# Graph network with five attention passes on one core: twelve places a slot for the block steps, typed products spread over them

## The chip, the cores and the metric

One NeuronCore of a Trainium2 chip runs the whole program in one launch. The metric is device time in microseconds (us); lower is better. Before the change it is 6849.43 us, the median of 3 runs (6848.14 to 6852.22).

## The reference

The inputs are 3125 nodes of 128 float32 features and 103,125 edges sorted by destination. Four graph layers run one after the other, each on relu(layernorm(x)) and each added to x:

```
L0: agg = segment_sum(edge_weight * h[src]); h' = leaky(( agg + h) W1 + b1 + (agg * h) W2 + b2)
L1: dot-product attention, 4 heads of 32, softmax over the edges of a destination, gate, layernorm
L2: GATv2 twice: score = att . leaky(xl[src] + xr[dst]); 4 heads of 32, then 1 head of 128
L3: heterogeneous transformer twice, 8 heads of 16, 8 node types, 8 edge relations:
    k, q, v = typed_linear(x, node_type, Wk | Wq | Wv)
    kw = rel_apply(k[src], edge_type, Watt);  m = rel_apply(v[src], edge_type, Wmsg)
    out = silu(typed_linear(segment_sum(softmax(kw . q[dst]) * m), node_type, Wa)), mixed with x, layernorm
```

So there is one weighted sum over the edges (pass 0) and five attention passes: pass 1 is L1, passes 2 and 3 are L2, passes 4 and 5 are L3.

## The kernel before

**Tiles, slots, passes.** The edges are cut into 830 tiles of 128, each with edges of one block of 128 destination nodes only; there are 25 blocks, so a block has 33.2 tiles on average. 16 tiles are a slot; a pass is 52 slots. In every pass POOL gathers the source rows of each tile by an indirect DMA (`gather_rows`, line 777), 830 a pass, into buffers that hold 3 slots (passes 1, 4, 5) or 4 slots (passes 2, 3). A buffer is free again when its rows are weighed (`exv_ready`).

**A slot in an attention pass** (`attention_pass`). Work on slot s overlaps the rest of slot s-1. Each engine goes through a fixed list written out in its own `slot()`:

- PE (tensor): `dst_rows` brings the destination side of four tiles to PSUM by the turned one-hots (L1280), in four groups 0 to 3; `own_rows` (L1289, GATv2 only) adds the gathered rows; `turn_scores` (L1295/L1299) turns the scores of slot s-1; `spread_drop` (L1304) and `turn_back` (L1309/L1311) serve the running softmax; `sums` (L1328) makes the per-tile sums in six units of 3 or 2 tiles (`SUMMED`).
- DVE (vector): `product` and `score` (L1098 to L1109) for the four groups; between `score` of the last group and the weighing lies the chain of scans over the slot's scores (L1115 to L1163), which waits for PE's turned scores and ScalarE's copy; `weigh` (L1176); `add` (L1188) adds sums to the accumulator.
- ACT (scalar): `keep_scores` (L1032), `open_scale` and `exps` (L1036, L1040), `exp_columns` (L1045), and in pass 3 the weighing of two of the four groups, `weigh_tiles` (L1053).
- SP (sync) loads the one-hots, their turned form and the flags, and issues the block steps' DMAs.

**Block steps.** When the last tile of a block is summed, the node work of that block follows (normalise, gate, layernorm, projections, write of the next pass's table). It is cut into steps d = 0, 1, 2 ... (classes `AfterL1`, `AfterGat`, `AfterGats`, `AfterTyped`, `AfterAll` for passes 1 to 5). A slot has `HOOKS` = 8 places on each engine, where `after.<engine>(x)` puts the step whose `first(k) + d` is x. A place is a position in the engine's instruction order, not a time. `first(k)` depends on where the block's last tile lies in its slot:

```
def first(self, k):
    s, t = divmod(last_tile(k), GT)
    return HOOKS * (s + 1) + 6 if t < ON_TIME else HOOKS * (s + 2)
```

`ON_TIME` is 11. Blocks 0 to 8 and 14 to 22 have t < 11; here they are called **early blocks** (step 0 at the seventh place of slot s+1). Blocks 9 to 13, 23 and 24 are **late blocks** (step 0 at the first place of slot s+2). Blocks are 2.07 slots apart, so each kind repeats nearly every two slots.

**Steps that matter.** Pass 3 (`AfterGats`): d = 3 statistics on DVE, d = 5 standard deviation on ACT (`deviation`, L1507: a square root and the activation table it needs), d = 6 its use on DVE (`standard`, L1513), d = 8 the turn on PE, d = 9 `by_type` on DVE (L2081), d = 11 key and value on PE (L2093), d = 12 query (L2100), d = 14, 16, 18, 20 the relation products (L2116), each taken by ACT one place later (L2138). Pass 4 (`AfterTyped`): d = 3 turn, d = 4 `by_type`, d = 5 output product (`layer_pe`, L2333), d = 12 `by_type`, d = 13 key, value and query together, d = 15 to 18 relation products.

## Time and profile before

| | |
|---|---|
| median of 3 runs | 6849.43 us |
| the profiled execution's own time | 6853.72 us |
| its span (first to last instruction) | 6851.4 us |
| busy: POOL, DVE, PE, ACT | 69%, 72%, 68%, 24% |
| mean granted TensorE clock | 0.766 |
| indirect gathers on POOL (L777) | 4980, about 0.95 us each |

The span is cut by the trace into stretches; "busy" is the time in which an engine had an instruction in it. A wait is the idle time of an engine just before an instruction, with what ended it behind the arrow. In the trace a float32 product of 128 columns shows as two records, so `x32` of L2093 is 16 products in the program.

### The profile page before, as it was taken

How to read it: one execution, taken by the hardware profiler on the slowest of the kernel's cores; microseconds unless marked ns; L12 is line 12 of the kernel's file. 1: busy time of each engine (PE TensorE's matmuls, PEld its weight loads, DVE VectorE, ACT ScalarE, POOL GpSimd, SP SyncE). 2: the span in 40 equal slices, each digit the busy share in tenths (PEclk: the TensorE clock that was granted, in tenths of full speed). 3: DMA queues.
4: the chain of work that ended last, by engine and by line, in shares of the span. 5: the costliest groups of instructions: out<-in, count | busy, mean ns of one | idle time of the engine just before them, and what ended most of it. 6: DMA issues, size and time to landing. Idle time of an engine off the chain costs nothing. (4 is left out here: it accounts for less than half of the span.)

```text
span 6851.4 us, 92813 instructions
## 1 busy us (share of the span) xinstructions
PE 4685.2 (68%) x26423; PEld 3967.3 (58%) x26423; DVE 4944.6 (72%) x14309; ACT 1666.6 (24%) x5319; POOL 4758.0 (69%) x4996
## 2 busy tenths in 40 slices
PE   2555555566666677877688788857787776676666
PEld 1444444555555466666566666646677675565655
DVE  4444443788888688888688778857777774888887
ACT  2433333122222111111133323312222221112121
POOL 3777776777777577777577777547667663777775
PEclk8676766777777788888789889967787776777777
DMA  4544444666666454545455555556667664666665
GB/s 129 171 158 162 160 159 150 209 216 211 215 210 207 128 168 156 168 156 168 135 177 189 182 164 189 170 167 223 218 223 230 211 211 129 227 219 227 219 226 157
DMA packets 407532, 1266.65 MB, mean 185 GB/s; under 512 B 128582, under 2 KB 189766, under 8 KB 320630
## 3 DMA queue, kind: packets, MB, share of 16 engines
q1 hardware_dynamic: 200000, 760.73, 30.3%
q0 software_dynamic: 199760, 495.12, 26.3%
q10 hardware_dynamic: 7270, 4.88, 0.3%
q8 instruction: 221, 3.62, 0.2%
q14 instruction: 281, 2.30, 0.1%
HBM read 1083.37 MB, written 176.98 MB: 184 GB/s over the span
## 5 line engine op out<-in xcount | busy, mean ns | idle before, releaser
L777 POOL DMA_INDIRECT gathered_rows<-table_l,arena x3048 | 2912.0, 955 | 1083.6 <-issue 911.5
L1188 DVE TENSOR_TENSOR acc<-acc,ps 128x136 f32 (+2 forms) x4160 | 1209.2, 291 | 517.4 <-PE ps L1328 354.3
L1280 PEld LDWEIGHTS ps<-dst_side,onehot_t 128*128 128x128 f32 x8320 | 1307.2, 235 | 445.7 <-issue 370.7
L1280 PE MATMUL ps<-dst_side,onehot_t 128*128 x8320 | 1416.8, 325 | 184.1 <-issue 106.9
L777 POOL DMA_INDIRECT gathered_rows<-table_l,src_rel_edges x1116 | 1061.3, 951 | 617.9 <-issue 330.6
L1328 PE MATMUL ps<-weighted_rows,onehot 128*128 128x136 f32 (+2 forms) x8320 | 1271.3, 314 | 14.8 <-DVE acc L1188 11.1
L1328 PEld LDWEIGHTS ps<-weighted_rows,onehot 128*128 128x128 f32 x8320 | 1215.4, 225 | 48.5 <-issue 38.4
L1109 DVE TENSOR_REDUCE scores<-products 128x16 f32<-128x512 f32 (+2 forms) x1040 | 711.5, 684 | 27.0
L900 PE MATMUL ps<-gathered_rows,onehot 128*128 128x128 f32 x1664 | 338.7, 367 | 473.3 <-ACT gathered_rows L837 471.4
L777 POOL DMA_INDIRECT arena<-table_l,src_rel_edges x544 | 517.9, 952 | 193.6 <-issue 161.8
L864 DVE TENSOR_TENSOR acc<-acc,ps 128x128 f32 x832 | 238.5, 287 | 535.8 <-PE ps L900 498.7
L900 PEld LDWEIGHTS ps<-gathered_rows,onehot 128*128 128x128 f32 x1664 | 292.8, 265 | 529.5 <-ACT gathered_rows L837 528.0
L1304 PE MATMUL ps<-open_node_drop,ones 64*128 64x4 f32 (+2 forms) x520 | 131.3, 323 | 513.1 <-DVE open_node_drop L1145 513.0
L1176 DVE TENSOR_TENSOR weighted_rows<-gathered_rows,ps 128x512 f32<-128x512 f32 x732 | 454.2, 679 | 5.4 <-ACT weighted_rows L1045 4.7
L1304 PEld LDWEIGHTS ps<-open_node_drop,ones 64*128 64x128 f32 (+2 forms) x520 | 111.0, 265 | 574.1 <-DVE open_node_drop L1145 570.9
L1289 PE MATMUL ps<-gathered_rows,ident 128*128 128x512 f32 x624 | 398.9, 725 | 42.7 <-DMA gathered_rows<-table_l,arena 42.6
L1104 DVE TENSOR_TENSOR products<-gathered_rows,ps 128x512 f32<-128x512 f32 x420 | 284.8, 678 | 139.0 <-DMA gathered_rows<-table_l,src_rel_edges 69.2
L837 ACT ACTIVATE gathered_rows<-gathered_rows,arena 128x128 f32<-128x128 f32 x832 | 264.9, 391 | 434.2 <-DMA gathered_rows<-table_l,arena 433.9
L777 POOL DMA_INDIRECT arena<-table_l,arena x272 | 258.6, 951 | 82.9 <-issue 80.7
L2116 PE MATMUL ps<-arena 32*128 32x256 f32 x800 | 268.9, 462 | 33.0 <-ACT arena L2138 31.3
L1309 PE MATMUL ps<-ident,exp_scores_t 64*128 64x64 f32 (+2 forms) x260 | 99.4, 382 | 272.2 <-ACT exp_scores_t L1040 272.2
L1102 DVE SCALAR_TENSOR_TENSOR products<-ps,vectors 128x512 f32<-128x512 f32 x312 | 210.8, 676 | 102.1 <-PE ps L1289 101.6
(321 smaller groups left out, 6208.1 us busy)
## 6 DMA issues: line engine op xcount, KB each, us to landing
onehot_t<-onehots_turned SPq DMA_DIRECT2D x260, 1024.0 KB
onehot<-onehots SPq DMA_DIRECT2D x260, 1024.0 KB
onehots<-onehot SPq DMA_DIRECT2D x52, 1024.0 KB, 6.6
onehots_turned<-onehot_t SPq DMA_DIRECT2D x52, 1024.0 KB, 4.3
table_l<-arena SPq DMA_DIRECT2D x50, 1024.0 KB
gathered_rows<-table_l,arena POOLq DMA_INDIRECT x3048, 2.5
segment_flags_sb<-segment_flags SPq DMA_DIRECT2D x1300, 8.2 KB
arena<-type_mask_rows SPq DMA_DIRECT2D x75, 256.0 KB
```

The lines of the kernel that those rows point to most:

```text
L777: pool.indirect_dma_start(out=home(v, t // GC)[:, t % GC, :], out_offset=None, in_=table, in_offset=bass.IndirectOffsetOnAxis(ap=index[:, ...
L837: ins = nc.scalar.activation(weighed[:, u, t, :], rv[:, u, t, :], ACT.Copy, scale=e.ewE[:, bass.ds(s * GT + t, 1)])
L900: ins = nc.tensor.matmul(ps[:, bank(u, j), g * P:g * P + D], e.oh[:, u, GC * j + g, :], weighed[:, u, GC * j + g, :], start=True, stop=True)
L1104: ins = V.tensor_tensor(out, home(v, j)[:, :, 0:D], z, ALU.mult)
L1109: V.tensor_reduce(scE[:, GC * j:GC * (j + 1), :], e.prod[:, j % 2, :].rearrange("p (g h d) -> p g h d", g=GC, h=H), AX, ALU.add).then_inc( ...
L1176: V.tensor_tensor(exvH[:, GC * j:GC * (j + 1), :, 0:hs], home(v, j)[:, :, vrow:vrow + D].rearrange("p g (h d) -> p g h d", h=H), bc(exE[:, ...
L1188: V.tensor_tensor(a, a, ps[:, BP + n % 3, at:at + PW], ALU.add).then_inc(e.acc_step.sem, 1)
L1280: ins = nc.tensor.matmul(ps[:, BZ + k, g * P:(g + 1) * P], e.ohT[:, u, t * P:(t + 1) * P], kRows[:, bass.ds(bs[t % 8], D)], start=not by_p ...
L1289: nc.tensor.matmul(ps[:, BZ + j % 2, :].rearrange("p (g d) -> p g d", d=D), e.ident[:, :], home(v, j)[:, :, 0:D], start=False, stop=True). ...
L1304: nc.tensor.matmul(dropP, e.onesF[0:LP, :], e.drop[0:LP, :, :].rearrange("p q h -> p (q h)")[:, 0:H], start=True, stop=True)\
L1328: ins = nc.tensor.matmul(ps[:, BP + n % 3, at:at + PW], e.oh[:, u, t, :], exvT[:, t, :], start=True, stop=True)
L2116: ins = mm(home, self.kvS[lane, m * P:(m + 1) * P], self.bd[lane, m * RELS * BAND:(m + 1) * RELS * BAND], start=True, stop=True)
```

## The change

`HOOKS` becomes 12: each slot has twelve places instead of eight. On PE they lie: places 0, 1 before `spread_drop`; 2 before `dst_rows` 2; 3 before the sums; 4 and 5 around `dst_rows` 3; 6 between sums units 4 and 5; 7, 8, then the first destination rows of the next slot, 9, 10 and, behind `own_rows` 3, 11. On DVE 0 and 1 precede the chain of scans, 2 the weighing, 3 `product` 1, 4 to 7 lie around the first adds, 8 after `score` 2, 9 and 10 after the adds of unit 3, 11 after `score` 3. On ACT 0 and 1 precede `open_scale`, 2 follows the weighing, 11 follows `keep_linear`. The steps keep their numbers up to the typed products; from there on they are renumbered. `first(k)` is 12 (s+1) + 9 for early blocks and 12 (s+2) for late ones. PE's `dst_rows` 0 of slot s+1 moves from the start of its slot to place 9 of slot s.

```diff
-HOOKS = 8
+HOOKS = 12
...
-                for h in range(3, 7):
+                for h in range(3, 11):
                     after.act(act, x + h)
...
-                if cur:
-                    bs = blocks_of(s, 0)
-                    e.oht_here[u].wait(pe, a_no, 16 * (q + 1))
-                    dst_rows(s, w, qw, 0, bs)
                 if chain:
                     turn_scores(r)
                 if cur:
                     own_rows(s, w, qw, 0)
-                    dst_rows(s, w, qw, 1, bs)
+                    dst_rows(s, w, qw, 1, first_places.pop(s))
...
+                after.pe(pe, x + 5)
                 if chain:
                     sums(r, v, 3)
-                after.pe(pe, x + 5)
+                    sums(r, v, 4)
+                after.pe(pe, x + 6)
                 if chain:
-                    sums(r, v, 4)
                     sums(r, v, 5)
-                after.pe(pe, x + 6)
+                after.pe(pe, x + 7)
+                after.pe(pe, x + 8)
+                if cur and ahead:
+                    first_dst_rows(s + 1, *place(w, qw, ways, 1))
+                after.pe(pe, x + 9)
+                after.pe(pe, x + 10)
                 if cur:
                     own_rows(s, w, qw, 3)
-                after.pe(pe, x + 7)
+                after.pe(pe, x + 11)
...
-        return HOOKS * (s + 1) + 6 if t < ON_TIME else HOOKS * (s + 2)
+        return HOOKS * (s + 1) + 9 if t < ON_TIME else HOOKS * (s + 2)
...
 class AfterGats(Typed):
             elif d == 11:
-                self.key_and_value(pe, k, k + 1)
+                self.key(pe, k, k + 1)
             elif d == 12:
+                self.key_or_value(1)
+            elif d == 13:
                 self.query(pe)
-            elif d in (14, 16, 18, 20):
-                self.relations(pe, k, (d - 14) // 2)
+            elif d in (15, 17, 19, 21):
+                self.relations(pe, k, (d - 15) // 2)
...
 class AfterTyped(FromLayer):
             elif d == 13:
-                self.key_and_value(pe, k, 2 * k + 2)
+                self.key(pe, k, 2 * k + 2)
+            elif d == 14:
+                self.key_or_value(1)
+            elif d == 15:
                 self.query(pe)
-            elif 15 <= d < 19:
-                self.relations(pe, k, d - 15)
+            elif d in (17, 19, 21, 23):
+                self.relations(pe, k, (d - 17) // 2)
```

ACT's steps that take these results move along by one or two numbers. Line numbers below the edits grow, by 5 in the pass and by 17 or more in the block steps (L1280 becomes L1285, L2093 becomes L2113, L2100 L2120, L2116 L2136, L1507 L1524, L1513 L1530).

**Place 1: PE, pass 3, an early block, around the turned scores.** L1295/L1297 (after: L1300/L1302) turn the scores; L2093 is key and value; L2113 in the change is key, then value; L2100/L2120 is the query; L1304/L1309 is `spread_drop`; L2116/L2136 a relation product. Before:

```order
L1280 MATMUL ps<-dst_side,onehot_t 128x128 x4
L1295 MATMUL ps<-ident,scores 16x128
L1297 MATMUL ps<-ident,linear_shares 16x128
L1289 MATMUL ps<-gathered_rows,ident 128x512
L1280 MATMUL ps<-dst_side,onehot_t 128x128 x4
L2093 MATMUL ps<-arena 128x128 x16
L1304 MATMUL ps<-open_node_drop,ones 128x1
L1309 MATMUL ps<-ident,exp_scores_t 128x16
L1311 MATMUL ps<-ident,segment_maxima 128x16
L2100 MATMUL ps<-arena 128x128 x8
```

With the change:

```order
L2113 MATMUL ps<-arena 128x128 x8
L728 TENSOR_LOAD tile_block
L745 ISA x3
L1285 MATMUL ps<-dst_side,onehot_t 128x128 x4
L2113 MATMUL ps<-arena 128x128 x8
L2120 MATMUL ps<-arena 128x128 x8
L1300 MATMUL ps<-ident,scores 16x128
L1302 MATMUL ps<-ident,linear_shares 16x128
L1294 MATMUL ps<-gathered_rows,ident 128x512
L1285 MATMUL ps<-dst_side,onehot_t 128x128 x4
L2136 MATMUL ps<-arena 128x256 x2
L1309 MATMUL ps<-open_node_drop,ones 128x1
```

Key and value stood between the turn of the scores and `spread_drop`, the query behind the turn back; now all three stand ahead of the turn of the scores, with the next slot's first destination rows after the key, and the first relation product stands ahead of `spread_drop`.

**Place 2: ACT and DVE, pass 3, the same block, around the weighing.** L1053 is ACT's weighing, L1507/L1524 the table load and square root of the deviation; L1176 is DVE's weighing, L1513/L1530 the use of the deviation, L1098 to L1109 product and score 1, L1188 adds. ACT before, then with the change:

```order
L1053 ACTIVATE weighted_rows<-gathered_rows,weighted_rows 128x128 x8
L2138 ACTIVATE arena<-ps 128x8x32 x2
L1507 ACT_TABLE_LOAD
L1507 ACTIVATE row_scalars<-row_scalars 128x1
L2227 ACTIVATE h_nodes<-x_nodes,row_scalars 128x128
L2229 ACTIVATE acc<-acc 128x136
```

```order
L1045 ACTIVATE weighted_rows<-ps 128x16
L1053 ACTIVATE weighted_rows<-gathered_rows,weighted_rows 128x128 x8
L1524 ACT_TABLE_LOAD
L1524 ACTIVATE row_scalars<-row_scalars 128x1
L2247 ACTIVATE h_nodes<-x_nodes,row_scalars 128x128
L2249 ACTIVATE acc<-acc 128x136
```

DVE before, then with the change:

```order
L1176 TENSOR_TENSOR weighted_rows<-gathered_rows,ps 128x4x128 x2
L1098 TENSOR_TENSOR products<-ps,gathered_rows 128x512
L1100 SCALAR_TENSOR_TENSOR products<-products,vectors 128x512
L1109 TENSOR_REDUCE scores<-products 128x4
L728 TENSOR_LOAD tile_block
L737 ISA x3
L1188 TENSOR_TENSOR acc<-acc,ps 128x130 x3
L1513 RECIPROCAL row_scalars<-row_scalars 128x1
L1514 SCALAR_TENSOR_TENSOR row_scalars<-row_scalars 128x1
```

```order
L1176 TENSOR_TENSOR weighted_rows<-gathered_rows,ps 128x4x128 x2
L1530 RECIPROCAL row_scalars<-row_scalars 128x1
L1531 SCALAR_TENSOR_TENSOR row_scalars<-row_scalars 128x1
L1098 TENSOR_TENSOR products<-ps,gathered_rows 128x512
L1100 SCALAR_TENSOR_TENSOR products<-products,vectors 128x512
L1109 TENSOR_REDUCE scores<-products 128x4
```

On ACT a relation copy has gone from between weighing and table load. On DVE the use of the deviation stood behind product 1, score 1 and three adds; now it follows the weighing at once.

**Place 3: PE, pass 4, an early block, typed products.** L1299/L1304 turns the scores, L2072/L2089 turns the nodes. Before:

```order
L1309 MATMUL ps<-ident,exp_scores_t 128x128
L728 TENSOR_LOAD tile_block
L745 ISA x3
L1280 MATMUL ps<-dst_side,onehot_t 128x128 x4
L2093 MATMUL ps<-arena 128x128 x16
L2100 MATMUL ps<-arena 128x128 x8
L1328 MATMUL ps<-weighted_rows,onehot 128x136 x8
L1280 MATMUL ps<-dst_side,onehot_t 128x128 x4
L1328 MATMUL ps<-weighted_rows,onehot 128x136 x3
L2116 MATMUL ps<-arena 128x256 x2
L1328 MATMUL ps<-weighted_rows,onehot 128x136 x5
L2116 MATMUL ps<-arena 128x256 x4
```

With the change:

```order
L2089 MATMUL ps<-ident,h_nodes 128x128
L728 TENSOR_LOAD tile_block
L745 ISA x3
L1285 MATMUL ps<-dst_side,onehot_t 128x128 x4
L2113 MATMUL ps<-arena 128x128 x16
L1304 MATMUL ps<-ident,scores 128x128
L1285 MATMUL ps<-dst_side,onehot_t 128x128 x4
L2120 MATMUL ps<-arena 128x128 x8
L1309 MATMUL ps<-open_node_drop,ones 128x8
L1314 MATMUL ps<-ident,exp_scores_t 128x128
L2136 MATMUL ps<-arena 128x256 x2
```

Key, value and query stood together ahead of the sums; now key and value stand ahead of the turn of the scores and the query behind `dst_rows` 1.

## Rows read from the trace of the kernel before

**Rows 1.** Busy time by stretch: first to last gather of passes 1 to 5 (columns: its first line).
```profile
core 0: us, PE busy (x) PEld busy (x) DVE busy (x) ACT busy (x) POOL busy (x), PEclk, DMA share, GB/s
1185.60:2227.90 1042.30, 659.57 (x3742) 586.69 (x3743) 845.07 (x2500) 232.71 (x702) 789.71 (x830) 0.72 0.64 213
2272.20:3311.60 1039.40, 813.17 (x4246) 629.86 (x4246) 841.19 (x2468) 140.31 (x604) 786.74 (x830) 0.84 0.52 163
3356.50:4412.20 1055.70, 842.42 (x5134) 694.17 (x5134) 863.78 (x2543) 324.16 (x1028) 799.28 (x830) 0.86 0.58 183
4522.60:5657.00 1134.40, 865.25 (x5205) 771.10 (x5205) 857.66 (x2311) 250.78 (x793) 789.26 (x830) 0.77 0.67 222
5760.40:6802.80 1042.40, 678.52 (x4022) 613.38 (x4023) 853.25 (x2336) 198.66 (x635) 789.79 (x830) 0.73 0.68 222
```
**Rows 2.** Waits of POOL's gathers for weighing (us in total, times, longest us).
```profile
POOL gathered_rows L777 <- DVE weighted_rows L1176: 87.6, 63, 6.0
```
**Rows 3.** One DVE instruction of each slot (L1163) in five windows: count, durations, first and last start.
```profile
L1163 DVE TENSOR_TENSOR scores_less_max<-scores_t,segment_maxima x52: 282/283/284, 2307.4 to 3332.4; 64x128 f32<-64x128 f32 x52
...
L1163 DVE TENSOR_TENSOR scores_less_max<-scores_t,segment_maxima x19: 278/279/280, 3429.0 to 3801.4; 16x128 f32<-16x128 f32 x19
...
L1163 DVE TENSOR_TENSOR scores_less_max<-scores_t,segment_maxima x11: 278/279/280, 3820.8 to 4060.7; 16x128 f32<-16x128 f32 x11
...
L1163 DVE TENSOR_TENSOR scores_less_max<-scores_t,segment_maxima x18: 291/292/292, 4638.0 to 5033.7; 128x128 f32<-128x128 f32 x18
...
L1163 DVE TENSOR_TENSOR scores_less_max<-scores_t,segment_maxima x10: 291/292/351, 5052.7 to 5247.4; 128x128 f32<-128x128 f32 x10
```
**Rows 4.** Timeline of pass 3, an early block: ScalarE's weighing, table load and square root.
```profile
4250.07 2.45 ACT L1053 ACTIVATE weighted_rows<-gathered_rows,weighted_rows 128x128 f32<-128x128 f32 x8
...
4250.33 1.27 DVE L1176 TENSOR_TENSOR weighted_rows<-gathered_rows,ps 128x512 f32<-128x512 f32 x2
...
4253.07 1.28 ACT L1507 ACT_TABLE_LOAD   x1
...
4254.36 0.20 ACT L1507 ACTIVATE row_scalars<-row_scalars 128x1 f32<-128x1 f32 x1
```
**Rows 5.** Timeline of pass 3, the same block: end of the slot and the typed products.
```profile
4257.65 0.69 DVE L1102 SCALAR_TENSOR_TENSOR products<-ps,vectors 128x512 f32<-128x512 f32 x1
...
4259.97 1.06 PE L1280 MATMUL ps<-dst_side,onehot_t 128*128 x8
...
4262.00 0.39 PE L1295 MATMUL ps<-ident,scores 128*16 128x128 f32 x2 [0.98 <-DVE scores L1109]
...
4264.39 3.74 PE L2093 MATMUL ps<-arena 128*128 128x128 f32 x32
...
4269.20 2.05 PE L2100 MATMUL ps<-arena 128*128 128x128 f32 x16
```
**Rows 6.** Timeline of pass 4, early blocks: PE's typed work and VectorE's waits.
```profile
4937.37 0.42 DVE L1115 TENSOR_TENSOR_SCAN tile_scans<-segment_flags_sb,scores_t 128x128 f32<-128x128 f32 x1 [2.99 <-ACT scores_t L1032]
...
4945.00 3.62 PE L2333 MATMUL ps<-arena 128*128 128x128 f32 x16
...
4949.48 2.74 DVE L1188 TENSOR_TENSOR acc<-acc,ps 128x136 f32 x8 [1.85 <-PE ps L1328]
...
4957.14 0.33 PE L1299 MATMUL ps<-ident,scores 128*128 128x128 f32 x1 [2.58 <-DVE scores L1109]
...
4966.21 5.18 PE L2093 MATMUL ps<-arena 128*128 128x128 f32 x32
...
4973.91 2.75 DVE L1188 TENSOR_TENSOR acc<-acc,ps 128x136 f32 x8 [5.03 <-PE ps L1328]
...
4976.55 1.13 PE L2116 MATMUL ps<-arena 32*128 32x256 f32 x4
```
**Rows 7.** Timeline of pass 2: own rows on PE, and VectorE's wait for the last of them.
```profile
3140.78 1.02 PE L1289 MATMUL ps<-gathered_rows,ident 128*128 128x512 f32 x2
...
3163.90 0.69 DVE L1102 SCALAR_TENSOR_TENSOR products<-ps,vectors 128x512 f32<-128x512 f32 x1 [2.31 <-PE ps L1289]
```

77 lines of the change are left out of this document (45 added, 32 removed).

## The prediction

> **What bounds the kernel now.** I read the stretches of the passes first. POOL issues its 830 gathers in 1042 us in passes 1 and 5, and in 1039 us in pass 2, whatever else goes on; only pass 3 (1056 us) and pass 4 (1134 us) take longer [rows 1]. So a gather costs 1.25 us of POOL's time, a slot of 16 costs 20.0, and two slots 40.1. Next the waits: POOL waits 87.6 us for weighing in the main buffers [rows 2], nearly all of it in pass 4. Then the period of the compute, by one VectorE instruction that comes once a slot [rows 3]. In pass 2 the compute goes at the gathers' pace (1025 us for 51 slots, 20.1 each). In pass 3 the early blocks take 372.4 us for 18 slots, which is 41.4 us for two slots; the late ones 239.9 us for 10, or 48.0. In pass 4 the early blocks take 395.7 us for 17, or 46.6, the late ones 194.7 for 9, or 43.3. The second run of early blocks repeats the first in both. Passes 3 and 4 are therefore bound by the chain of PE and VectorE, passes 1 and 5 by POOL, and pass 2 stands at the border. What the change is worth is decided by the two-slot periods of passes 2, 3 and 4, with 40.1 us as the floor.
>
> How an early block of pass 4 loses its time [rows 6]: VectorE waits 5.03 us for the sums, because key, value (5.18 us) and query (about 2 us) stand ahead of them; 1.85 us in the other slot, because the output product (3.62 us) does; and 2.99 us for the turned scores, behind relation products of 1.13 us. These move by some tenths from pair to pair (I take 9.0 in all). Early blocks of pass 3 lose about 2 us only: there key and value (3.74 us) start at 4264.39, just behind the turned scores, and run under VectorE's scans [rows 5].
>
> **The change, part by part.** I go by two slots (one block) and count VectorE's new waits less the old ones.
>
> *Pass 3, early blocks, deviation.* ScalarE weighs from 4250.07 to 4252.52, then would load the table (1.28) and take the root (0.20): 4254.0. VectorE's second weighing ends at 4251.60 [rows 4]. The use of the deviation now follows there (place 2), so VectorE stands still for 2.4 us; now it comes behind product 1, score 1 and three adds, where nothing waits. Queued behind it are product 1 and all adds. Cost +2.4. The row shows the root 0.01 us behind the load's end. The Trainium skill, "ScalarE: Activation LUTs", section "What ACT_TABLE_LOAD costs", gives the load 1283 ns and a drain of 1380 ns besides; with that drain on the path this term would be 3.8, but the row has none, so I keep 2.4.
>
> *Pass 3, early blocks, typed products.* `by_type` now ends just ahead of product 2. From product 2's start (4257.65) VectorE needs 4.3 us to the end of score 3, which frees the turn of the scores at 4262.00 [rows 5]. PE has to do key, first destination rows, value and query before that turn (place 1): 3.74 + 1.06 + 2.05, and 0.3 for loading the block numbers, 7.1 us. The turn is late by 2.8 us. Everything behind it (ScalarE's copy, the scans, weighing) is late with it. Cost +2.8. Next, the first relation product and its copy now come ahead of `spread_drop` and ScalarE's table load: destination rows, product (1.13), a copy (some 0.7, estimated from VectorE's 0.69 for as many columns) and load (1.28) end about 0.9 us after the scans want the exponent. Cost +0.9. Against this the old 2 us of waits (sums late behind relation products at a cold PE, `spread_drop` late behind key and value) shrink by about 1.3. Sum: +4.8 us for two slots, 17 such pairs: +82.
>
> *Pass 3, late blocks.* The wait of 4 to 5 us behind key and value goes, and three smaller ones come (value and query ahead of `spread_drop`, 1.9; relation products ahead of the sums, 1.6 and 1.3; relations ahead of the turn, 1.5). I get 7.5 us against 9.0: -1.5, five pairs, -8.
>
> *Pass 4, early blocks.* Key and value, now 5.2 us at the clock of [rows 6] or 3.7 at that of [rows 5], lie ahead of the turn of the scores, where product and score 3 cover 1.4: 2.4 us late (from 2.2 to 3.8). The output product moves ahead of `dst_rows` 2, still ahead of the sums, and `by_type`, which covered part of it, moves to the other side of the chain: 2.4 instead of 1.85. The query behind `dst_rows` 1 costs 0.4. The relation products at places 2, 4, 6 and 8 put 4.5 us into one slot; PE has some 2.6 us to spare before the turn [rows 6], so 0.5, 0.4 and 1.5 remain. Sum 7.6 to 7.9 against 9.0: -1.2, 17 pairs, -20. Late blocks: value and query still ahead of the sums (2.3), three relations ahead of the turn (3.1), others 1.1: 6.5 against some 5.8, +0.7, five pairs, +3.
>
> *Pass 2.* First destination rows now precede the last own rows (1.02 us each) [rows 7]. They wait for product 2, so product 3 gets its rows about 1 us later in each slot that has nothing between. `linear_share` moves to place 7 ahead of product 2, where it waits 2.1 us for the projection; in return the 2.31 us wait shrinks to about 0.9 [rows 7]. Two slots become 1.2 us longer with early blocks (17 pairs) and 2 with late ones (five). That would be +30; part lies beside the gathers, which set the pace there: I take +20, between 0 and +35.
>
> *At no cost.* Passes 0, 1 and 5: pass 0 has its own places; in 1 and 5 the gathers are the bound, with 2 to 3 us for two slots to spare; were that gone, each added us would cost 20. The ends of the passes keep their chain of steps, since block 24 starts after the loop either way. SP's writes come at a place where the turned one-hots two slots ahead wait for PE anyway. First destination rows ahead of the turn save nothing in passes 4 and 5 where PE had the time free.
>
> Sum: 82 - 8 - 20 + 3 + 20 = +77 us. Against the profiled execution (6853.7) that is 6931; the median of the runs is 4.3 lower, so I predict **6927**.
>
> **Bounds.** For pass 3's early blocks the terms could be 3 (only the table load, if PE hides the rest) to 7 (products at pass 4's speed): +45 to +120. Pass 4: from -65 (the turn less late and the relations hidden, -4 for two slots) to +40. Pass 2: 0 to +35. Together the forecast's own range is 6880 to 6985.
>
> **Rivals.** *A, faster: the pieces fit.* PE stands idle 2.6 us before the turn in pass 4 when no step is there [rows 6], and a piece of 16 records is 1.9 to 2.6 us. If value and relations really find PE idle, pass 4's early pairs fall by 5 us (-85), the late ones by 2.5 (-12), pass 3's late ones by 5 (-25). Pass 3's early blocks would still pay the deviation (+2.4, +41). Net -80: 6769. For it: the 5.03 us wait is real and its cause is taken apart. Against it: all pieces fall into the same short stretch ahead of the turn. It decides if the turn is late by under 1 us.
>
> *B, even.* Pass 4 gains 60 (-3.5 for two slots) and passes 2 and 3 lose that much: 6849, within 0.2%. For it: pass 4 has the most waits to give. Against it: as for A.
>
> *C, much slower: the clock.* PE's granted clock is 0.86 of full in pass 3 and 0.77 in pass 4 [rows 1]; 32 records took 3.74 us in one and 5.18 in the other, where PE had stood idle before [rows 5, 6]. If the new waits of VectorE leave PE at 1.2 GHz when the products come, key, value and query take up to 3.6 us each instead of 1.9, all of it ahead of the turn: +5 us more for two slots in pass 3, +3 in pass 4, 17 pairs each: 6927 + 136 = 7063. The Trainium skill, "TensorE: Matmul & The Clock Gate", section on the clock gate, has activity release the throttle, so work spread thinner would meet the lower clock more; no row here shows which side the spread pieces fall on. Against it: they come right behind the sums, with PE warm.
>
> *D, the change does nothing there:* the steps do move in the order lists, so I give this no chance.
>
> **Chances.** Forecast 0.68, A 0.15, B 0.10, C 0.07. 0.2% of this kernel is 14 us, about what a measurement can tell from no change. Of the forecast, 0.02 lies within it. Faster 0.16, same 0.11, slower 0.73. The range for 8 in 10 leaves out most of A below and C above: 6835 to 6990.
>
> **What would show it.** Pass 3's early pairs at 45 to 47 us instead of 41.4, with a wait of VectorE's reciprocal (L1530) for ScalarE of about 2.4, and one of the scans for the copied scores of 2 to 3. Pass 4's early pairs at 44 to 46.5, the wait of 5.03 for the sums gone, one of 2 to 3 at the scans in both slots. POOL's waits now in pass 3 too; passes 1 and 5 still at 1042 us. I am wrong if pass 3's early pairs stay under 43, or pass 4's fall below 43.

## The result, and the profile after

The changed kernel takes **6948.18 us** (median of 4 runs, 6946.21 to 6951.05), the kernel before in runs beside it 6848.78 us (6842.28 to 6852.22). The ratio is 1.0144, 95% interval 1.0129 to 1.0158: **slower by 99 us**. The forecast was 6927 us, range 6835 to 6990.

Stretches from the first to the last gather of passes 2 to 4, as in [rows 1], in the profiled execution of the changed kernel (columns as there):

```profile
2271.80:3310.40 1038.60, 775.13 (x4203) 589.50 (x4204) 832.86 (x2436) 143.91 (x601) 785.91 (x830) 0.89 0.51 162
3367.80:4527.00 1159.20, 900.76 (x5136) 742.33 (x5136) 864.07 (x2529) 325.36 (x1029) 799.24 (x830) 0.83 0.51 165
4644.30:5753.30 1109.00, 850.06 (x5227) 764.02 (x5228) 860.43 (x2297) 248.66 (x789) 786.35 (x829) 0.82 0.68 227
```

Passes 1 and 5 take 1040 and 1042 us as before. Between first and last gather only passes 3 and 4 have moved: pass 3 from 1056 to 1159 us, pass 4 from 1134 to 1109. The wait behind the last gather counts too, so the table further down goes from the first gather of a pass to the first of the next: pass 2 from 1084 to 1096, pass 3 from 1166 to 1277, pass 4 from 1238 to 1211. That is +12 + 110 - 27 = +95, against +93 between the two spans (6851.4 and 6944.2).

POOL's waits for weighing, 87.6 us before [rows 2], in the same view:

```profile
POOL gathered_rows L777 <- DVE weighted_rows L1176: 178.2, 84, 6.2
```

The instruction that comes once a slot [rows 3], in early blocks of pass 3 and of pass 4:

```profile
L1163 DVE TENSOR_TENSOR scores_less_max<-scores_t,segment_maxima x17: 278/279/280, 3485.2 to 3865.4; 16x128 f32<-16x128 f32 x17
...
L1163 DVE TENSOR_TENSOR scores_less_max<-scores_t,segment_maxima x19: 291/292/293, 4717.6 to 5116.1; 128x128 f32<-128x128 f32 x19
```

Two slots take 380.2 / 8 = 47.5 us in pass 3's early blocks (41.4 before), 48.4 in its late ones (11 of them from 3887.1 to 4129.3; 48.0 before), 44.3 in pass 4's early ones (46.6 before) and 44.9 in its late ones (9 from 5136.1 to 5315.5; 43.3 before).

Where VectorE stands still in pass 3 (line, what it waits for: us in total, times, longest). The changed kernel:

```profile
DVE acc L1188 <- PE ps L1333: 71.7, 69, 3.3
DVE tile_scans L1115 <- ACT scores_t L1032: 56.0, 46, 2.4
DVE row_scalars L1530 <- ACT row_scalars L1524: 44.0, 17, 2.6
```

The kernel before, the same view of its pass 3 (the deviation does not appear there):

```profile
DVE acc L1188 <- PE ps L1328: 57.4, 52, 5.3
...
DVE tile_scans L1115 <- ACT scores_t L1032: 9.8, 32, 1.4
```

These views end with the last gather, where pass 3 has grown by 104 us (1055.7 to 1159.2), and these rows hold that: 44.0 for the deviation, 46.2 for turned scores that come late, 14.3 for sums that come late. The same in pass 4, first changed, then before:

```profile
DVE tile_scans L1115 <- ACT scores_t L1032: 105.1, 41, 3.8
DVE acc L1188 <- PE ps L1333: 27.7, 21, 2.8
```

```profile
DVE acc L1188 <- PE ps L1328: 129.8, 49, 5.2
DVE tile_scans L1115 <- ACT scores_t L1032: 55.6, 23, 3.4
```

There 102.1 us of waiting for sums went, and 49.5 us for turned scores came. The stretch is only 25 us shorter, since smaller waits grew by about 24 us in all, such as those of L1176 for ScalarE's columns (1.7 to 9.1) and those at L1188 that no engine ended (2.4 to 14.5).

Inside one early block of pass 3 of the changed kernel (timeline: start, duration, engine; in brackets the idle time before and what ended it):

```profile
3654.57 1.28 ACT L1524 ACT_TABLE_LOAD   x1
3655.86 0.20 ACT L1524 ACTIVATE row_scalars<-row_scalars 128x1 f32<-128x1 f32 x1
3656.10 0.16 DVE L1530 RECIPROCAL row_scalars<-row_scalars 128x1 f32<-128x1 f32 x1 [2.63 <-ACT row_scalars L1524]
...
3666.30 0.69 DVE L1109 TENSOR_REDUCE scores<-products 128x4 f32<-128x512 f32 x1
...
3667.40 1.95 PE L2120 MATMUL ps<-arena 128*128 128x128 f32 x16
3669.28 0.39 PE L1300 MATMUL ps<-ident,scores 128*16 128x128 f32 x2
...
3670.23 0.41 DVE L1115 TENSOR_TENSOR_SCAN tile_scans<-segment_flags_sb,scores_t 16x128 f32<-16x128 f32 x1 [2.39 <-ACT scores_t L1032]
```

Both waits are those that the sum was built on: the root behind weighing and load, and the turn of the scores at 3669.28, 2.29 us after score 3 ended (3666.99), behind the query.

### The profile page after: what moved, and what is told of

Its sections match the earlier page's. It is cut to its first block and busy times, and to the rows that moved or that the text cites. A ratio compares the mean times of both kernels' runs of the same rounds, so it can differ in the third digit from the quotient of the medians.

```text
span 6944.2 us, 92831 instructions
## 1 busy us (share of the span) xinstructions
PE 4691.6 (68%) x26423; PEld 3980.8 (57%) x26423; DVE 4967.0 (72%) x14309; ACT 1718.7 (25%) x5355; POOL 4757.0 (69%) x4996
## 3 DMA queue, kind: packets, MB, share of 16 engines
q8 instruction: 221, 3.62, 0.2%
## 5 line engine op out<-in xcount | busy, mean ns | idle before, releaser
L1285 PE MATMUL ps<-dst_side,onehot_t 128*128 x8320 | 1400.1, 323 | 226.8 <-issue 120.7
L1285 PEld LDWEIGHTS ps<-dst_side,onehot_t 128*128 128x128 f32 x8320 | 1287.1, 233 | 462.2 <-issue 376.0
L1188 DVE TENSOR_TENSOR acc<-acc,ps 128x136 f32 (+2 forms) x4160 | 1208.8, 291 | 369.2 <-PE ps L1333 174.4
L1333 PE MATMUL ps<-weighted_rows,onehot 128*128 128x136 f32 (+2 forms) x8320 | 1332.9, 322 | 41.1 <-DVE acc L1188 32.8
L1333 PEld LDWEIGHTS ps<-weighted_rows,onehot 128*128 128x128 f32 x8320 | 1266.9, 232 | 91.8 <-issue 57.7
L1109 DVE TENSOR_REDUCE scores<-products 128x16 f32<-128x512 f32 (+2 forms) x1040 | 711.4, 684 | 27.0
L1309 PE MATMUL ps<-open_node_drop,ones 64*128 64x4 f32 (+2 forms) x520 | 127.3, 315 | 644.4 <-DVE open_node_drop L1145 644.2
L1309 PEld LDWEIGHTS ps<-open_node_drop,ones 64*128 64x128 f32 (+2 forms) x520 | 105.2, 252 | 705.6 <-DVE open_node_drop L1145 704.8
L1176 DVE TENSOR_TENSOR weighted_rows<-gathered_rows,ps 128x512 f32<-128x512 f32 x732 | 454.8, 680 | 17.2 <-ACT weighted_rows L1045 15.4
L1294 PE MATMUL ps<-gathered_rows,ident 128*128 128x512 f32 x624 | 377.2, 689 | 24.8 <-DMA gathered_rows<-table_l,arena 24.8
L1036 ACT ACTIVATE open_node_scale<-ps,open_node_column 128x4 f32<-128x4 f32 (+2 forms) x260 | 68.8, 265 | 897.0 <-PE ps L1309 896.6
```

Of the source, the lines that this page charges most:

```text
L1109: V.tensor_reduce(scE[:, GC * j:GC * (j + 1), :], e.prod[:, j % 2, :].rearrange("p (g h d) -> p g h d", g=GC, h=H), AX, ALU.add).then_inc( ...
L1176: V.tensor_tensor(exvH[:, GC * j:GC * (j + 1), :, 0:hs], home(v, j)[:, :, vrow:vrow + D].rearrange("p g (h d) -> p g h d", h=H), bc(exE[:, ...
L1188: V.tensor_tensor(a, a, ps[:, BP + n % 3, at:at + PW], ALU.add).then_inc(e.acc_step.sem, 1)
L1285: ins = nc.tensor.matmul(ps[:, BZ + k, g * P:(g + 1) * P], e.ohT[:, u, t * P:(t + 1) * P], kRows[:, bass.ds(bs[t % 8], D)], start=not by_p ...
L1294: nc.tensor.matmul(ps[:, BZ + j % 2, :].rearrange("p (g d) -> p g d", d=D), e.ident[:, :], home(v, j)[:, :, 0:D], start=False, stop=True). ...
L1309: nc.tensor.matmul(dropP, e.onesF[0:LP, :], e.drop[0:LP, :, :].rearrange("p q h -> p (q h)")[:, 0:H], start=True, stop=True)\
```

## The experiments

Each was timed against the kernel before. All numbers by pass are from the profiled executions: first gather of the pass to the first of the next.

| kernel | median us | ratio to before (95%) | pass 2 | pass 3 | pass 4 |
|---|---|---|---|---|---|
| before | 6849 to 6854 | 1 | 1084 | 1166 | 1238 |
| the change | 6948.2 | 1.0144 (1.0129 to 1.0158) | 1096 | 1277 | 1211 |
| b1_dev | 6909.5 | 1.0085 (1.0068 to 1.0102) | 1086 | 1220 | 1239 |
| a1_dev | 6902.7 | 1.0075 (1.0058 to 1.0091) | 1099 | 1235 | 1211 |
| a2_typed3 | 6950.2 | 1.0145 (1.0128 to 1.0162) | 1098 | 1280 | 1214 |
| a3_typed4 | 6938.1 | 1.0128 (1.0111 to 1.0145) | 1100 | 1280 | 1199 |
| a4_dst | 6992.6 | 1.0195 (1.0178 to 1.0213) | 1083 | 1289 | 1258 |
| c1_typed_dst | 7000.1 | 1.0207 (1.0190 to 1.0224) | 1085 | 1297 | 1259 |
| a6_agg | 6945.0 | 1.0133 (1.0116 to 1.0149) | 1100 | 1280 | 1200 |
| c2_all | 6920.6 | 1.0096 (1.0079 to 1.0113) | 1082 | 1256 | 1219 |
| d2_type | 6895.4 | 1.0064 (1.0048 to 1.0081) | 1086 | 1269 | 1181 |
| d1_best | 6709.9 | 0.9793 (0.9776 to 0.9809) | 1085 | 1133 | 1133 |
| e1_typed | 6791.6 | 0.9906 (0.9889 to 0.9923) | 1086 | 1204 | 1141 |
| e2_rel | 6848.2 | 0.9995 (0.9985 to 1.0005) | 1081 | 1221 | 1177 |

### b1_dev and a1_dev: the deviation, put in and taken out

b1_dev puts the one wait into the kernel before; a1_dev takes it out of the changed one.

The edit of b1_dev, then that of a1_dev (`AfterGats.dve`):

```diff
-            elif d == 6:
+            elif d == 5:
                 self.standard(dve, c, k, "std").then_inc(S["scale"], 1)
```

```diff
-            elif d == 6:
+            elif d == 7:
                 self.standard(dve, c, k, "std").then_inc(S["scale"], 1)
```

> The kernel before, with one part of the change alone: in pass 3 VectorE's use of the deviation follows the weighing at once, ahead of product 1. Theory (VectorE stands still for table load and root, and nothing behind takes the time up): early pairs of pass 3 from 41.4 us to 43.8 (+2.4), late ones as before, passes 1, 2, 4 and 5 as before; 17 x 2.4 = +41, so 6890 us. Rival (the wait only takes the place of later waits of the same slot, such as those for the sums): early pairs stay within 0.7 us, 6849 to 6861.

> The changed kernel, with VectorE's use of the deviation in pass 3 one place later (d = 7: behind product 1 and score 1). Theory: the wait of 2.63 us at L1530 goes and nothing takes its place; early pairs of pass 3 from 47.7 to 45.1 us, 17 x 2.6 = -44, so 6904 us. Rival (the turn of the scores and the sums are late by PE anyway, VectorE waits there instead): early pairs stay at 47 or more, 6936 to 6948.

b1_dev: +58 us where +41 was expected, pass 3 +54, nothing elsewhere; VectorE waits 52.5 us at L1513, in 17 places. One of them:

```profile
3591.70 0.63 ACT L2138 ACTIVATE arena<-ps 128x256 f32<-128x256 f32 x2
3592.34 1.28 ACT L1507 ACT_TABLE_LOAD   x1
...
3593.87 0.16 DVE L1513 RECIPROCAL row_scalars<-row_scalars 128x1 f32<-128x1 f32 x1 [3.16 <-ACT row_scalars L1507]
```

The wait is 3.16 and not 2.4 since in this order a relation copy (0.63) still stands ahead of the load, which the change had moved. Behind it the waits for sums fall by 22.0 us in the pass (57.4 to 35.4), as the rival has it, and those at L1169 rise by 9.0. a1_dev: 45.5 us faster than the change, as expected; the 44.0 us at L1530 fall to 9.3, 10.7 us come for `by_type` (L2098 behind the turn of the nodes), and waits for the sums fall by 14. So this term is shown from both sides, 58 us put in and 45 taken out; part of the wait does take the place of others, so neither number is the wait alone.

### a2_typed3: the typed products of pass 3 behind the turn of the scores

`typed` gives late blocks the same places as early ones; below it `AfterGats.pe`. ScalarE takes each result one place behind.

```diff
+    def typed(self, k, d):
+
+        late = last_tile(k) % GT >= ON_TIME
+        return d + 3 if late and d >= 12 else d
...
-            elif d == 11:
+            elif self.typed(k, d) == 15:
                 self.key(pe, k, k + 1)
-            elif d == 12:
+            elif self.typed(k, d) == 16:
                 self.key_or_value(1)
-            elif d == 13:
+            elif self.typed(k, d) == 17:
                 self.query(pe)
-            elif d in (15, 17, 19, 21):
+            elif self.typed(k, d) in (19, 21, 23, 25):
```

> The changed kernel, in pass 3 alone with key and value behind the turn of the scores, the query ahead of destination rows 2, relation products at places 4, 6, 8 and 10, for early and late blocks. Theory (the late turn of the scores costs 2.4 us in a pair, relation products ahead of the table load and the sums another 1 to 1.9): early pairs from 47.7 to 44.5 us, late ones from 48.5 to about 46, 17 x 3.2 + 5 x 2.5 = -67, so 6881 us; the wait of 2.63 at L1530 stays. Rival (PE has too much in that slot wherever the pieces stand): the wait moves to spread_drop or to the sums, early pairs stay at 47, 6935 to 6948.

No gain, as in the rival (6950.2 us, its range ended at 6948). The wait for sums fell from 71.7 to 9.1 us, but:

```profile
DVE acc L1169 <- ACT open_node_scale L1036: 68.0, 22, 3.3
```

The chain of it in one block:

```profile
3669.84 0.60 PE L1300 MATMUL ps<-ident,scores 128*16 128x128 f32 x2 [2.40 <-DVE scores L1109]
...
3670.80 2.08 PE L1294 MATMUL ps<-gathered_rows,ident 128*128 128x512 f32 x2
...
3672.67 1.92 PE L1285 MATMUL ps<-dst_side,onehot_t 128*128 x8
...
3674.38 4.27 PE L2118 MATMUL ps<-arena 128*128 128x128 f32 x32
...
3679.29 0.29 DVE L1169 TENSOR_TENSOR acc<-acc,open_node_scale 128x129 f32 x1 [3.16 <-ACT open_node_scale L1036]
```

In the kernel before the same three cost 1.13, 1.05 and 3.74 us, and PE had been idle for 0.98 us before the turn (turn, key and value: [rows 5]). Here it had been idle for 2.40, and own rows and destination rows take about twice as long: that is the lower of PE's two clock levels (1.2 for 2.4 GHz; the granted clock is 0.50 of full from 3669.90 to 3674.30, and 1.00 in the same rows of the kernel before). Own rows, destination rows, key and value are 2.35 us longer together, which is most of the 3.16 us that `open_node_scale`, behind `spread_drop` (the matmul that L1036 reads), comes late.

### a4_dst and c1_typed_dst: the first destination rows back, alone and on top of a2_typed3

```diff
+                if cur:
+                    first_dst_rows(s, w, qw)
                 if chain:
                     turn_scores(r)
...
                 after.pe(pe, x + 8)
-                if cur and ahead:
-                    first_dst_rows(s + 1, *place(w, qw, ways, 1))
```

> The changed kernel, with the first destination rows back at the start of their own slot, right ahead of the turn of the scores; places and typed products stay. Theory (moving them cost pass 2 about 0.5 us a slot through the later own rows, and did nothing in passes 3 and 4, where the same products stand ahead of the turn in both orders): pass 2 gets its 12 us back (first to last L1163 from 1039 us to about 1027), pass 3 and 4 within 5 us, so about 6936. Rival 1 (in passes 3 and 4 the rows filled time in which PE stood idle): each slot 0.5 to 1 us longer, 6960 to 6990. Rival 2 (the rows ahead of the turn keep PE's clock up at the turn): passes 3 and 4 shorter by 10 to 30 us, 6910 to 6925.

> The kernel of a2_typed3 (key and value of pass 3 behind the turn of the scores), and the first destination rows back ahead of that turn. In a2_typed3 PE stood idle 2.4 us before the turn, and then the own rows took 2.08 us, destination rows 1 1.92 and key and value 4.27; the kernel before has 1.13, 1.05 and 3.74 there, with destination rows 0 right ahead of the turn. Theory (the clock: PE falls to the lower level in the idle stretch that the moved rows leave): own rows and destination rows back to 1.1 us each, key and value to 3.8, the wait of 3.1 us at L1169 falls to under 1, early pairs of pass 3 from 47.8 to 45.2; with pass 2's 12 us about 6890. Rival (the order alone: spread_drop is late behind 3.7 us of products in any case): early pairs stay at 47 or more, about 6938.

Pass 2 did what was expected (1096 to 1083 us). The rest did not: a4_dst is 44 us slower than the change, with +48 in pass 4 and +12 in pass 3. The same place of pass 4, first the change, then a4_dst:

```profile
4883.93 1.13 PE L1285 MATMUL ps<-dst_side,onehot_t 128*128 x8 [0.81 <-DVE products L1104]
4886.10 3.84 PE L2113 MATMUL ps<-arena 128*128 128x128 f32 x32 [1.04 <-DVE arena L2098]
...
4890.40 0.42 DVE L1115 TENSOR_TENSOR_SCAN tile_scans<-segment_flags_sb,scores_t 128x128 f32<-128x128 f32 x1 [2.18 <-ACT scores_t L1032]
```

```profile
4889.90 5.47 PE L2112 MATMUL ps<-arena 128*128 128x128 f32 x32 [2.98 <-DVE arena L2097]
4895.21 1.06 PE L1285 MATMUL ps<-dst_side,onehot_t 128*128 x8
...
4896.72 0.42 DVE L1115 TENSOR_TENSOR_SCAN tile_scans<-segment_flags_sb,scores_t 128x128 f32<-128x128 f32 x1 [4.69 <-ACT scores_t L1032]
```

In the changed kernel the rows stand in the middle of an idle stretch, which becomes 0.81 and 1.04 us. Without them PE is idle for 2.98 us at a time, key and value take 5.47 instead of 3.84, and the rows' own 1.06 comes on top, all ahead of the turn: 4.69 us of waiting for 2.18, in every pair of early blocks. That is rival 1: in pass 4 the rows had filled idle time. Rival 2 expected the clock to be kept by rows right ahead of the turn; here it falls in the stretch that they have left. c1_typed_dst, meant to give the clock back in pass 3, did not (7000.1 us, 6890 expected): PE finished the rows early and then still stood idle 2.4 us for score 3, with own rows at 2.08. The waits at L1169 fell from 68.0 to 51.6 us, and those for turned scores rose from 52.9 to 87.3. So the place of these rows did not decide PE's clock in pass 3.

### a3_typed4 and a6_agg: pass 4

a3_typed4 makes the edit of a2_typed3 in `AfterTyped`. a6_agg moves the aggregation on ScalarE by one place (with turn, `by_type` and output product behind it):

```diff
-            if d == 2:
+            if d == self.AGG:
                 act.wait_ge(S["norm"], k + 1)
```

`AGG` is 3 in `AfterTyped` and stays 2 in `AfterAll`.

> The changed kernel, with the same move in pass 4 alone (key and value behind the turn of the scores, query ahead of destination rows 2, relation products at places 4, 6, 8 and 10). PE stands idle 4 us there in the other slot, between the turn of the nodes and spread_drop. Theory: the wait of 2.6 us for the turned scores goes, spread_drop comes 0.8 late, the query costs 0.8 more ahead of the sums than a relation product did, the last relation product ahead of the next turn 0.3: early pairs from 44.3 to 43.3 or less, 17 x 1 to 1.5 = -17 to -26, so about 6927 us. Rival (key and value ahead of spread_drop cost as much as ahead of the turn): 44.3 or more, 6948 to 6960.

> The changed kernel, in pass 4 alone with the aggregation of the block (ScalarE, 8 + 1 instructions of 2.1 us together, L2321 and after) behind the copy of the turned scores instead of ahead of it, its turn, by_type and the output product one place later each. Theory (the wait of 2.17 us for the copied scores, in the slot without typed products ahead of the turn, is ScalarE's and not PE's): that wait falls to 0.3, the sums wait as before, early pairs of pass 4 from 44.3 to about 42.4, 17 x 1.9 = -32, 6916 us. Rival (PE's relation products and destination rows ahead of the turn set it): the wait stays at 2 or more, 6944 to 6950.

a3_typed4 gained 11 us in pass 4, less than the 17 at least of its expectation: the waits for turned scores fell from 105.1 to 76.0, those for `open_node_scale` rose from 4.7 to 28.5. a6_agg gained 10 us there, a third of what was expected, and 3 us in the whole run. The 2.17 us that its expectation names is the wait of the slot with key and value, and it stayed; the slot with relation products, where the aggregation stands, has 2.69 in the change. In a6_agg it is gone, about 1.5 or about 2.5 to 2.7 us, and in the case of 2.74 the sums before it had run at the lower clock (granted 0.54; 1.00 in the other block shown):

```profile
4859.50 2.02 PE L1333 MATMUL ps<-weighted_rows,onehot 128*128 128x136 f32 x16
...
4901.11 3.62 PE L1333 MATMUL ps<-weighted_rows,onehot 128*128 128x136 f32 x16
...
4914.00 0.49 DVE L1115 TENSOR_TENSOR_SCAN tile_scans<-segment_flags_sb,scores_t 128x128 f32<-128x128 f32 x1 [2.74 <-ACT scores_t L1032]
```

So two things held the same scan, ScalarE's aggregation and PE; taking one away frees it only where the other is absent.

### c2_all: all of these edits together

The edits of a1_dev, a2_typed3, a3_typed4, a4_dst and a6_agg, with `linear_share` of pass 2 at d = 12 for 10.

> The changed kernel with all these edits: deviation one place later in pass 3; typed products behind the turn of the scores in passes 3 and 4; first destination rows back ahead of the turn; the aggregation behind the copied scores in pass 4; linear_share of pass 2 behind the adds (d = 12). Theory (the waits add up, nothing else binds): early pairs of pass 3 from 47.7 to 42.5, late ones from 48.5 to 46, pass 4's early pairs from 44.3 to 42, late ones to 43, pass 2 back by 15: 88 + 12 + 39 + 4 + 15 = -158, about 6790 us, under the kernel before. Rival (a wait that goes lets the next one in, as in a2_typed3): half of it, 6870.

28 us faster than the change, where 158 were expected: worse than the rival's half. Pass 3 pays about 4 us at L1115 in most pairs of early blocks and 5.8 in late ones, where relation products and first destination rows now stand together ahead of the turn. The pieces do not add up; each was worth what the next wait in the slot allowed.

### d2_type and d1_best: by_type behind score 3, then the places of the kernel before

c1_typed_dst had one thing left that differed from the kernel before between the sums and the turn: `by_type` ahead of product 2. Both kernels here leave the first destination rows where the change has them in passes 1, 4 and 5, and put them back in passes 2 and 3; both hold the edits of a3_typed4 and a6_agg in pass 4 and `linear_share` at d = 12 in pass 2.

d2_type (`typed` now shifts from d = 11 on; `AfterGats.dve`, then PE's slot):

```diff
-            elif d == 9:
+            elif self.typed(k, d) == 14:
                 self.by_type(dve, k + 1, k, "q_done", k)
...
-                if cur and ahead:
+                if cur and ahead and not gat:
                     first_dst_rows(s + 1, *place(w, qw, ways, 1))
```

d1_best besides, in `AfterGats` (ScalarE's takes move along):

```diff
-            elif d == 6:
+            elif d == 8:
                 self.standard(dve, c, k, "std").then_inc(S["scale"], 1)
...
-            if d == 8:
+            if d == 10:
                 self.turn(pe, self.e.hN[:, k, :], "h_made", k, "rel_taken", BANDS * k)
...
-            elif self.typed(k, d) in (19, 21, 23, 25):
+            elif self.typed(k, d) in (19, 22, 27, 29):
```

and in `AfterTyped`:

```diff
-            elif d == 12:
+            elif self.typed(k, d) == 14:
                 self.by_type(dve, 2 * k + 2, k, "y_made", k + 1)
...
-            elif self.typed(k, d) in (19, 21, 23, 25):
+            elif self.typed(k, d) in (19, 21, 23, 27):
```

> In pass 3 the kernel of c1_typed_dst (typed products behind the turn of the scores, first destination rows ahead of it), with one thing moved: by_type on VectorE from ahead of product 2 to behind score 3, where the kernel before has it. In c1_typed_dst PE ran through the sums under by_type, then stood idle 2.4 us before the turn of the scores, and own rows took 2.08 us. Theory (by_type's place makes the idle stretch, and the clock falls in it): the idle time before the turn falls to about 1 us, own rows to 1.1 us, key and value to 3.8, the wait at L1169 from 1.9 to under 0.7, and by_type covers the 0.6 us for the copied scores; early pairs of pass 3 from 47.8 to 45.3 (the 2.6 us for the deviation stay). Rival (the order of PE alone): 47 or more. In pass 4: typed products behind the turn of the scores and the aggregation behind its copy together, first destination rows ahead: by a3_typed4 and a6_agg 44.3 less 2, 42.3 for an early pair. In pass 2: first destination rows back and linear_share behind the adds, at the gathers' pace. About 6948 - 41 - 34 - 13 = 6860 us.

> As d2_type, and in pass 3 every step at the place that answers to that of the kernel before (deviation used behind the adds of unit 0, turn of the nodes behind the sums, two relation products ahead of the turn of the scores and two behind it), with late blocks' typed products at the same places as early ones. Theory (all of pass 3's loss is in those places, none in the number of places): early pairs of pass 3 at 41 to 42 us as in the kernel before, late ones 45 to 46 against 48.0 there. In pass 4 by_type stands behind score 3 too and the last relation product behind the turn of the scores: early pairs 41.5. Together 6948 - 102 - 12 - 48 - 13 = about 6775 us, under the kernel before. Rival (something else of the twelve places costs, or each wait removed lets in the next): early pairs of pass 3 at 44 or more, 6850 us or more.

d2_type: pass 3 gives 28 us back against c1_typed_dst, two thirds of what was expected of `by_type`. The idle time before the turn falls only to 1.83 us; own rows go down to 1.17 us, but the destination rows behind them still took 1.92: the granted clock is 1.00 from 3612.22 to 3613.60 and 0.50 from 3613.80 to 3616.80. Early pairs stay at 47, the rival's number, so for pass 3 only the direction holds. Pass 4 (1181) gains 30 of 34. The whole run takes 6895.4 us, 6860 expected.

d1_best is **6709.9 us, 2.07% faster than the kernel before** and 3.4% faster than the change. Its passes 3 and 4, first to last gather:

```profile
3356.00:4408.20 1052.20, 864.99 (x5274) 707.98 (x5275) 883.26 (x2597) 331.81 (x1060) 799.55 (x829) 0.87 0.58 186
4488.70:5530.50 1041.80, 807.33 (x5237) 721.28 (x5237) 864.77 (x2313) 251.61 (x794) 789.23 (x829) 0.85 0.72 242
```

Pass 4 goes at the gathers' pace for the first time. Pass 3's early pairs take 40.9 us, and its waits for the turned scores fall back to 9.6 us in 28 times.

It came out 65 us below its own expectation, about 30 in pass 3 and 30 in pass 4.

### e1_typed and e2_rel: d1_best with one part put back in each pass

e1_typed, `AfterGats.pe` (`by_type` back to d = 9, the deviation to 7), then `AfterTyped.pe`:

```diff
-            if d == 10:
+            if d == 8:
                 self.turn(pe, self.e.hN[:, k, :], "h_made", k, "rel_taken", BANDS * k)
-            elif self.typed(k, d) == 15:
+            elif d == 11:
                 self.key(pe, k, k + 1)
-            elif self.typed(k, d) == 16:
+            elif d == 12:
                 self.key_or_value(1)
-            elif self.typed(k, d) == 17:
+            elif d == 13:
                 self.query(pe)
...
-            elif self.typed(k, d) in (19, 21, 23, 27):
+            elif self.typed(k, d) in (19, 21, 23, 25):
```

e2_rel, `AfterGats.pe`, then `AfterTyped.dve`:

```diff
-            elif self.typed(k, d) in (19, 22, 27, 29):
+            elif self.typed(k, d) in (19, 22, 23, 25):
...
-            elif self.typed(k, d) == 14:
+            elif d == 12:
                 self.by_type(dve, 2 * k + 2, k, "y_made", k + 1)
```

> The kernel of d1_best with, in pass 3, key, value and query back at the changed kernel's places (ahead of the turn of the scores, for early blocks), and by_type ahead of product 2, the turn of the nodes and the use of the deviation one or two places earlier, which that order needs; relation products stay two ahead of the turn and two behind it. Theory (products ahead of the turn delay the scores by what VectorE does not cover, 2.4 us by the changed kernel's wait, 0.6 more for the deviation, 0.6 for the cover that by_type no longer gives): early pairs of pass 3 from 40.9 to 44 us, 17 pairs, +50. Rival (only the relation products' places mattered): 41.5 or less. In pass 4 the last relation product goes back ahead of the turn of the scores (place 10), by_type stays behind score 3. Theory (what stands ahead of the turn is paid there): early pairs of pass 4 from 41.0 to 42, POOL waits again, +15. Rival (by_type's place alone brought d1_best's gain over d2_type in pass 4): pass 4 stays. About 6710 + 50 + 15 = 6775 us.

> The kernel of d1_best with, in pass 3, all four relation products ahead of the next turn of the scores (places 4, 7, 8 and 10) instead of two ahead and two behind. Theory (four products of 1.13 us with their copies do not fit between the sums and the turn: in d2_type VectorE waited 2.1 to 3.8 us for the copied scores and 1.75 at L1169 behind them): a wait of 2 us or more at L1115 returns, early pairs from 40.9 to 43.5, late ones too, 22 x 2.6 = +57. Rival (the deviation and the turn of the nodes made d1_best's gain over d2_type in pass 3): 41.5 or less. In pass 4 by_type goes back ahead of product 3 (place 9), the last relation product stays behind the turn. Theory (by_type then no longer covers the turn of the scores, 0.6 us in a pair, and PE has more idle time before it): early pairs 41.0 to 41.6, +5 to +15. Rival (by_type's place brought d1_best's gain in pass 4): 42.3. About 6775 us.

Pass 3: typed products ahead of the turn cost 3.4 us for two slots (44.3 for 40.9, with a wait of 2.54 at L1115), all four relation products ahead of it 3.4 as well (44.3). Of the first, about 1.3 are not the products: 0.6 is the deviation, used one place earlier, and 0.7 `by_type`, which waits for the turned nodes. The passes grew by more than expected, by 71 us (50) and 89 (57), since late pairs grew too, from 42.7 us to 44.5 and 47.9. The second needs only a look at PE, which waits for each copy before the next product:

```profile
3570.04 2.07 PE L2144 MATMUL ps<-arena 32*128 32x256 f32 x4 [0.75 <-ACT arena L2166]
3572.05 2.08 PE L1285 MATMUL ps<-dst_side,onehot_t 128*128 x8
...
3575.42 0.41 DVE L1115 TENSOR_TENSOR_SCAN tile_scans<-segment_flags_sb,scores_t 16x128 f32<-16x128 f32 x1 [4.59 <-ACT scores_t L1032]
```

Pass 4: the last relation product ahead of the turn costs 8 us of the pass (1141 for 1133), about half the forecast. `by_type` ahead of product 3 costs 44 (1177) where 5 to 15 were forecast, so here the rival is right and `by_type`'s place made most of d1_best's gain over d2_type. So both runs missed their 6775 us, e1_typed by 17 and e2_rel by 73. The turn of the scores and what follows in pass 4, e2_rel, then d1_best:

```profile
4809.80 0.47 PE L1304 MATMUL ps<-ident,scores 128*128 128x128 f32 x1 [2.33 <-DVE scores L1109]
4810.07 1.92 PE L1285 MATMUL ps<-dst_side,onehot_t 128*128 x8
...
4811.78 5.61 PE L2121 MATMUL ps<-arena 128*128 128x128 f32 x32
...
4817.85 0.30 DVE L1169 TENSOR_TENSOR acc<-acc,open_node_scale 128x136 f32 x1 [2.32 <-ACT open_node_scale L1036]
```

```profile
4721.48 0.33 PE L1304 MATMUL ps<-ident,scores 128*128 128x128 f32 x1 [1.23 <-DVE scores L1109]
4721.64 1.82 PE L1285 MATMUL ps<-dst_side,onehot_t 128*128 x8
...
4723.25 4.65 PE L2121 MATMUL ps<-arena 128*128 128x128 f32 x32
...
4728.50 0.30 DVE L1169 TENSOR_TENSOR acc<-acc,open_node_scale 128x136 f32 x1 [0.20 <-ACT open_node_scale L1036]
```

With `by_type` behind score 3, VectorE reaches the scores 1.2 us sooner, PE is idle for 1.23 us instead of 2.33, key and value take 4.65 instead of 5.61, and `by_type` itself runs where VectorE would wait for the copied scores.

## Why the prediction was right, and where its steps were not

The total was right (+77 forecast, +99 measured, in the range), and so was the place: pass 3 loses, pass 4 gains, passes 1 and 5 stay at 1040 to 1042 us. By its own steps:

- **Deviation, +2.4 for two slots: right.** 2.63 us, 17 times, 44.0 us in all; put in alone it costs 58 us with the relation copy (b1_dev), taken out alone it gives 45 (a1_dev). The root starts 0.01 us behind the load's end in the rows of both kernels, and in the changed kernel the load starts 0.01 us behind the weighing (3652.11 to 3654.56). The Trainium skill gives a drain of 1380 ns beside the load in "ScalarE: Activation LUTs", section "What ACT_TABLE_LOAD costs"; the trace does not bear it out here: with it the wait would have been 4.0 us, an estimate from the page's figure.
- **Typed products ahead of the turn, +2.8: right.** The wait at L1115 is 2.39 us, and +46 us in pass 3; e1_typed, which puts them there in the best kernel, costs 3.4 for two slots with the 0.6 for the deviation and the 0.7 for `by_type`. That these products could simply go back behind the turn was a tacit part of this reading, and a2_typed3 shows it false by itself: `spread_drop` then comes 3.16 us late.
- **First relation product, +0.9: too high.** It shows as 0.22 us at L1169 and 0.57 at L1173; both lines together gained 9 us in the pass.
- **Old waits, -1.3: wrong, and the largest error.** "The old 2 us of waits ... shrink by about 1.3": the waits for sums rose by 14.3 us in pass 3 instead. The old one (1.34 us in a pair) did go, as in b1_dev, because VectorE now waits for the deviation meanwhile. But in the slot of the relation products three came, of 1.35, 0.36 and 1.27 us in a pair, where the kernel before has 0.28. The changed kernel, then the one before:

```profile
3677.47 2.08 PE L1285 MATMUL ps<-dst_side,onehot_t 128*128 x8
3679.34 3.39 PE L1333 MATMUL ps<-weighted_rows,onehot 128*128 128x130 f32 x16
3680.89 0.94 DVE L1188 TENSOR_TENSOR acc<-acc,ps 128x130 f32 x3 [1.35 <-PE ps L1333]
...
3686.44 0.94 DVE L1188 TENSOR_TENSOR acc<-acc,ps 128x130 f32 x3 [1.27 <-PE ps L1333]
```

```profile
4271.09 1.06 PE L1280 MATMUL ps<-dst_side,onehot_t 128*128 x8
4271.98 1.96 PE L1328 MATMUL ps<-weighted_rows,onehot 128*128 128x130 f32 x16
...
4277.65 0.94 DVE L1188 TENSOR_TENSOR acc<-acc,ps 128x130 f32 x3 [0.28 <-PE ps L1328]
```

  PE does not start late: its destination rows begin 1.25 us after VectorE's weighing (1.46 before). They and the sums take 5.2 us instead of 2.9, at a granted clock of 0.53 from 3675.50 to 3682.70 (1.00 from 4269.20 to 4273.90 before). In the kernel before, key, value and query kept PE busy up to these rows; the change took them away, PE stood idle for 1.87 us behind `spread_drop`, and single relation products follow. In a2_typed3, with the query in that place again, the same two take 1.06 and 1.96 us, and all waits for sums 9.1 us.
- **Late blocks of pass 3, -8: about +2.** 48.4 for 48.0. The new waits that the prediction lists add up to 6.3 us, not to its 7.5, so its own terms would have given a still larger gain.
- **Pass 4, -17: right in sign, -27, but with a wrong composition.** The turn late by 2.4: 2.18. Early pairs fell by 2.3 us instead of 1.2, late ones rose by 1.6 instead of 0.7. "First destination rows ahead of the turn save nothing in passes 4 and 5 where PE had the time free" was wrong: a4_dst shows 48 us for pass 4. Without those rows the change would have made pass 4 slower by 20 us (1258 for 1238), not faster. That idle time of PE is not free here, because the clock falls in it, was argued in rival C only for the new waits of VectorE, not for this move.
- **Pass 2, +20: +12.** All of it is the first destination rows (1083 without them); moving `linear_share` cost nothing beside the gathers.
- **Rival C.** Its mechanism is real (32 records take 3.74 to 5.61 us in these rows, on the whole longer behind longer idle time), and in pass 3 it made the new waits for sums above. Its price did not come: key, value and query ran at full clock ahead of the turn (2.05, 1.95 and 1.95 us; granted 1.00 from 3664.70 to 3669.20), right behind the sums as its "against" has it. Over the whole pass the granted clock fell from 0.86 to 0.83 in pass 3 and rose from 0.77 to 0.82 in pass 4. It also decided how well the remedies worked. The Trainium skill, "TensorE: Matmul & The Clock Gate", section "Part 1: The HAM clock gate (the "warmup" mystery)", has activity release the throttle; the trace agrees in direction, with 1.00 behind 0.98 us of idle time and 0.50 behind 2.40 us.
- **Signs.** Pass 3's early pairs came at 47.5 us, just over the 45 to 47 that were named; pass 4's at 44.3, within 44 to 46.5.
- **Rivals A and B.** The scans waited 2.39 us for the turned scores in pass 3 and 2.18 and 2.69 in the two slots of pass 4, so "the pieces fit" fell; d1_best shows that they do fit once they stand on both sides of the turn.

Still open: the parts of d1_best in pass 3 (turn of the nodes later, deviation used behind the first adds) were not run one by one, and no run shows why the clock of d2_type falls only when turn and own rows are done.

## What to carry to other kernels

A list of places cut finer does not make work fit: what counts is whether a piece lies ahead of the one instruction that the critical engine waits for (here the turn of the scores), and the same pieces gave +99 or -141 us by such choices. Put work that needs other engines' answers (a relation product and its copy) on both sides of that point, and put the critical engine's own side work (`by_type`) where it would wait anyway. Before taking a filler out of an idle stretch, look at how long the stretch becomes and at the duration of what follows it.
